# Generator blocks moved into the step, other first steps, and biases added tile by tile

## The reference

```
scale = cond @ norm_w.T + 1.0
h = x * (scale[:, None, :] * rsqrt(mean(x * x, -1) + 1e-6))
val, gate = split(h @ up_w.T, 2)                      # 2 x 1024 columns
h = val * gelu(gate)
y = act_quant(h) @ weight_quant(down_w).T + x         # rows to 8 bits, weights to -1, 0, 1

dWd = ((cond @ Wdd.T + bdd) * 0.1).reshape(B, 128, 256)
dWu = ((cond @ Wdu.T + bdu) * 0.1).reshape(B, 256, 128)
down = relu(y @ (Wd + dWd).T + bd)                    # weights of its own for each sequence
out = y + down @ (Wu + dWu).T + bu
```

## Time and profile before

| | us |
|---|---|
| median of three runs | 473.36 |
| the profiled execution, whole | 473.57 |
| its span, first to last instruction | 471.8 |
| PE busy in the span | 464.3 (98%) |
| VectorE busy | 386.4 (82%) |
| ScalarE busy | 364.3 (77%) |
| GpSimd busy | 269.1 (57%) |

### The profile page before, as it was taken

One profiled execution on the slowest core, in us unless ns is written; L12 is line 12 of the kernel. 1 busy time (PEld: TensorE's weight loads), 2 busy tenths in 40 slices (PEclk: granted clock), 3 DMA queues, 4 the chain that ended last, 5 costly groups with the idle time before them and its releaser, 6 DMA issues.

```text
span 471.8 us, 10035 instructions
## 1 busy us (share of the span) xinstructions
PE 464.3 (98%) x3276; PEld 269.3 (57%) x3276; DVE 386.4 (82%) x787; ACT 364.3 (77%) x636; POOL 269.1 (57%) x681
## 2 busy tenths in 40 slices
PE   8999999999999999999999999999999999999996
PEld 7445565665656555555555555555555555655564
DVE  3887798888989898788888887878888888777886
ACT  3788999999999967776777777686686787677664
POOL 1653558565675645465656546656555656544663
PEclk9999999999999999999999999999999999999999
DMA  7925588967778455535545445645535455444343
GB/s 259 392 80 111 135 206 200 260 182 217 182 236 243 104 103 120 106 100 162 130 133 157 91 124 136 166 122 136 137 84 162 124 145 147 113 105 119 101 81 110
DMA packets 118003, 70.99 MB, mean 150 GB/s; under 512 B 102016, under 2 KB 102976, under 8 KB 115904
## 3 DMA queue, kind: packets, MB, share of 16 engines
q1 hardware_dynamic: 117360, 69.63, 56.4%
q10 hardware_dynamic: 592, 0.73, 0.5%
HBM read 37.44 MB, written 8.39 MB: 97 GB/s over the span
## 4 chain that ended last, share of the span: by engine, by line
PE 91%; DVE 3%; DMA 1%; issue 1%; ACT 1%; POOL 1%; ACTq 0%; DVEq 0%; POOLq 0%
PE bank L1147 65%; PE bank L1161 11%; PE bank L1223 5%; PE bank L1255 4%; PE bank L1241 4%; DMA xT_s<-in_xT 1%; PE bank L1123 1%; PE bank L1129 1%; DVE up_lo L1020 0%; ACT gel L621 0%; DVE hid L857 0%; POOL nwt L463 0%; PE bank L1173 0%; DVE amax L865 0%; POOL rms L470 0%
## 5 line engine op out<-in xcount | busy, mean ns | idle before, releaser
L621 ACT ACTIVATE gel<-bank,rms 128x512 f32<-128x512 f32 x125 | 85.5, 685 | 87.3 <-PE bank L1147 84.4
L1147 PE MATMUL bank<-up_hi,xs_hi 128*128 128x512 f16 x492 | 146.3, 379 | 0.3 <-DVE hid L857 0.3
L1147 PE MATMUL bank<-up_lo,xs_hi 128*128 128x512 f16 x492 | 146.3, 379 | 0.0
L1147 PE MATMUL bank<-up_hi,xs_lo 128*128 128x512 f16 x492 | 146.3, 379 | 0.0
L857 DVE SCALAR_TENSOR_TENSOR hid<-bank,rms,gel 128x512 f32<-128x512 f32 x121 | 90.6, 749 | 62.3 <-ACT gel L621 61.5
L1147 PEld LDWEIGHTS bank<-up_lo,xs_hi 128*128 128x128 f16 x492 | 48.1, 98 | 58.1
L1147 PEld LDWEIGHTS bank<-up_hi,xs_lo 128*128 128x128 f16 x492 | 48.1, 98 | 58.0
L448 POOL TENSOR_TENSOR wsplit<-stage,wsplit 128x288 f16<-128x288 f32 x64 | 53.1, 859 | 42.1 <-ACT wsplit L593 42.1
L865 DVE TENSOR_REDUCE amax<-hid 128x1 f32<-128x1024 f32 x61 | 74.4, 1220 | 2.1
L634 ACT ACTIVATE hid<-hid,amax 128x1024 f32<-128x1024 f32 (+1 forms) x62 | 70.0, 1130 | 0.4 <-DVE amax L909 0.4
L1161 PE MATMUL bank<-tern,qT 128*128 128x256 bf16 x504 | 65.3, 273 | 0.8 <-DVE x L969 0.7
(11 more groups left out here) (145 smaller groups left out, 662.7 us busy)
## 6 DMA issues: line engine op xcount, KB each, us to landing
xn_s<-in_xn SPq DMA_DIRECT2D x32, 256.0 KB, 3.4
stage<-in_WddT SPq DMA_DIRECT2D x8, 1024.0 KB, 6.1
stage<-in_WduT SPq DMA_DIRECT2D x8, 1024.0 KB, 5.4
xT_s<-in_xT SPq DMA_DIRECT2D x31, 256.0 KB, 3.1
out<-out_s SPq DMA_DIRECT2D x30, 256.0 KB, 2.3
adapt<-in_up_wT SPq DMA_DIRECT2D x4, 512.0 KB, 7.8
x<-in_down_wT SPq DMA_DIRECT2D x2, 512.0 KB, 9.1
qT<-qn SPq DMA_TRANSPOSE x63, 2.7
```

What stands on the lines that cost most here:

```text
L621: nc.scalar.activation(gel_of(t, c), u_banks(t, c)[1][:], ACT.Gelu, scale=rms[:, t // TPB % XN_SLOTS, t % TPB:t % TPB + 1]).then_inc(gelu_ ...
L1147: ins = nc.tensor.matmul(dst[:], a[:, t // TPB % 2, k, cols], w[:, c, k, v, :], start=(k == 0 and n == 0), stop=(k == KD - 1 and n == 2))
```

## The change

The step loop of PE issues `generate(q)` between `down` and `up(s, 1)`, and in step 7 + q rather than at the end of step 6 + q. In the first two steps, `up_first` is cut in two: the passes with the weights' low parts become `up_first_end` and come later. Eleven idle matmuls stand ahead of the first real one rather than eight. The sum of the absolute weights moves from step 3 to step 2, with ACT's `absolute_sum`, DVE's `ternary_first` and `ternary_second` earlier; `squares(2)`, `squares(3)` and `rsqrt_guess(2)` are earlier as well. `base_sum` on POOL moves from the start to step 5. The first load of `xT` goes from ACT's queue to SP's, behind the first piece of the up weights. At the end, `output(B - 3)` on PE moves ahead of three transposes, `total(B - 3)` on DVE with it, and POOL adds the bias of sequence B - 2 one tile at a time, the first of them earlier.

```diff
@@ -69,7 +69,7 @@
 N_NEWTON = 11
 
 
-IDLE_FIRST = 8
+IDLE_FIRST = 11
 IDLE_SECOND = 7
 
 
@@ -395,6 +395,8 @@
             sp.dma_start(cond2[0:C, :], condT).then_inc(ld_cond, 16)
             for n in range(NC * KD):
                 sp.dma_start(raw_up[:, n // KD, n % KD], up_wT[:, n // KD, n % KD]).then_inc(ld_up[n], 16)
+                if n == 0:
+                    sp.dma_start(xT_s[:, 0], xT[0]).then_inc(ld_xT[0], 16)
             sp.dma_start(xn_s[:, 0], xn[0]).then_inc(ld_xn[0], 16)
             load_x(1)
             for i in range(2):
@@ -511,6 +513,12 @@
                     nc.gpsimd.tensor_tensor(out_s[:, b % OUT_SLOTS, i], x1[:, (b * TPB + i) % X1_SLOTS], bu_row[:], ALU.add
                                             ).then_inc(outb_done, 1)
 
+            def output_bias_tile(b, i):
+                pool.wait_ge(x1_done, b * TPB + i + 1)
+                pool.wait_ge(stored[b % OUT_SLOTS], 16 * (b // OUT_SLOTS))
+                nc.gpsimd.tensor_tensor(out_s[:, b % OUT_SLOTS, i], x1[:, (b * TPB + i) % X1_SLOTS], bu_row[:], ALU.add
+                                        ).then_inc(outb_done, 1)
+
             def base_sum():
                 pool.wait_ge(ld_base, 16 * N_BASE)
                 nc.gpsimd.tensor_scalar(bias_raw, bias_raw, DELTA_SCALE, None, ALU.mult).then_inc(base_ready, 1)
@@ -545,7 +553,6 @@
 
             split_cond()
             rsqrt(1)
-            base_sum()
             rsqrt(2)
             for t in range(FIRST - 2):
                 dequantization(t)
@@ -559,6 +566,8 @@
                     low_part(q)
                 for b in scales(s):
                     rsqrt(b)
+                if s == FIRST + 1:
+                    base_sum()
                 if s == LAST_T - 1:
                     residual_low(LAST_T - 4)
                 for b in adapter_splits(s):
@@ -567,11 +576,12 @@
                     identity()
             output_bias(B - 3)
             dequantization(LAST_T - 1)
+            output_bias_tile(B - 2, 0)
             residual_low(LAST_T - 3)
             middle_low(B - 4)
             dequantization(LAST_T)
             residual_low(LAST_T - 2)
-            output_bias(B - 2)
+            output_bias_tile(B - 2, 1)
             middle_low(B - 3)
 
             pool.wait_ge(x1_lo_done, LAST_T - 2)
@@ -697,7 +707,6 @@
                                          scale=1.0 / A_SCALE).then_inc(relu_done, 1)
 
             act.dma_start(normw, norm_wT).then_inc(ld_cond, 16)
-            act.dma_start(xT_s[:, 0], xT[0]).then_inc(ld_xT[0], 16)
             act.dma_start(cond2[C:2 * C, :], condT).then_inc(ld_cond_again, 16)
             act.wait_ge(const_ready, 2)
             nc.scalar.activation(warm[:], zero[:], ACT.Gelu)
@@ -715,18 +724,18 @@
             squares(0)
             scaled_high(1)
             squares(1)
+            absolute_sum(0)
             gelu(0, 0)
             gelu(0, 1)
             gelu(1, 0)
+            absolute_sum(1)
             gelu(1, 1)
-            absolute_sum(0)
-            absolute_sum(1)
+            squares(2)
             gelu(2, 0)
             quantize(0)
             quantized(0)
             gelu(2, 1)
             scaled_high(2)
-            squares(2)
             gelu(3, 0)
             quantize(1)
             quantized(1)
@@ -738,8 +747,8 @@
                     relu(b)
                 gelu(s, 0)
                 if s == FIRST:
+                    squares(3)
                     gelu(s, 1)
-                    squares(3)
                 quantize(s - 1)
                 if s < LAST_T:
                     for t in split_tiles(s):
@@ -1029,16 +1038,16 @@
             quant_scale(0)
             gate(1, 0)
             gate(1, 1)
+            ternary_first()
             gate(2, 0)
+            rsqrt_guess(2)
             quant_scale(1)
             gate(2, 1)
-            ternary_first()
+            ternary_second()
             gate(3, 0)
-            rsqrt_guess(2)
             scaled_low(2)
             quant_scale(2)
             gate(3, 1)
-            ternary_second()
             ternary_third()
             for s in range(FIRST, NT):
                 if s == LAST_T:
@@ -1083,9 +1092,9 @@
             residual_high_last()
             residual_low(LAST_T)
             residual_low(LAST_T - 1)
+            total(B - 3)
             x63_lo_evacuate()
             x62_evacuate()
-            total(B - 3)
             split_last()
             total(B - 2)
             total_last()
@@ -1122,6 +1131,10 @@
                         for v, dst in enumerate(u_banks(t, c)):
                             nc.tensor.matmul(dst[:], a[:, 0, k, cols], up_hi[:, c, k, v, :],
                                              start=(k == 0 and n == 0), stop=False)
+
+            def up_first_end(t, c):
+
+                cols = slice(t * P, (t + 1) * P)
                 for k in range(KD):
                     if t == 0:
                         pe.wait_ge(up_ready, c * KD + k + 1)
@@ -1288,17 +1301,24 @@
                 if s < TPB:
 
                     up_first(0, s)
+                    if s == 1:
+                        up_first_end(0, s)
                     up_first(1, s)
+                    if s == 0:
+                        up_first_end(0, s)
+                    up_first_end(1, s)
                     continue
-                if s == 3:
+                up(s, 0)
+                if s == 2:
 
                     pe.wait_ge(hid_done, NC + 1)
                     pe.wait_ge(absum_ready, 2)
                     nc.tensor.matmul(sum_ps, ones[:], wsum[:, 0:1], start=True, stop=False)
                     nc.tensor.matmul(sum_ps, ones[:], wsum[:, 3:4], start=False, stop=True).then_inc(absum_full, 1)
-                up(s, 0)
                 for t in downs(s, 0):
                     down(t)
+                for q in chunk(s, 2):
+                    generate(q)
                 if s < LAST_T:
                     up(s, 1)
                 else:
@@ -1306,8 +1326,6 @@
                     up_last(1)
                 for t in downs(s, 1):
                     down(t)
-                for q in chunk(s, 1):
-                    generate(q)
                 for b in outputs(s):
                     output(b)
                 for b in sequences(s, 0):
@@ -1320,6 +1338,7 @@
             down_last()
             pe.wait_ge(late_lo_done, 3)
             x_transpose(LAST_T - 2, x61_ps, (0, 1))
+            output(B - 3)
 
             pe.wait_ge(last_x1_hi_done, 1)
             x_transpose(LAST_T, x63_hi_ps, (0,))
@@ -1328,7 +1347,6 @@
             x_transpose(LAST_T, x63_lo_ps, (1,))
             pe.wait_ge(x1_lo_done, LAST_T - 2)
             x_transpose(LAST_T - 1, x62_ps, (0, 1))
-            output(B - 3)
             middle_last(1)
             middle_last(0)
             output(B - 2)
```

## The result

The changed kernel takes 481.11 us (median of four runs, 480.92 to 482.01), the kernel before, beside it, 473.41. The ratio is 1.0166, with a 95% interval of 1.0149 to 1.0184: slower by 7.7 us, where +4.5 was forecast and the range ended at 479.4. The profiled execution of the changed kernel took 480.92 us with a span of 479.2; before, 473.57 and 471.8.

A forecast was written before the change was run, and what follows sets the result against it. PE, busy for 98% of the span, was taken as the bound. The terms 6.7 - 0.8 - 1.15 - 0.3 = +4.5 us took the profiled 473.57 to 478.1, so 477.9 us was predicted, range 476.2 to 479.4.

The forecast's parts named there:

- The chain behind the third pass: PE waits for `xs_lo` in tiles 8 to 22, T ending the previous even step's second half: eight times, 6.7 us.
- The 0.84: PE's forecast wait for `xs_lo` at each third pass, in us, from T + 8.31 to T + 9.15.
- the 0.13: Forecast delay in us from the end of `xs_lo` until PE goes on.
- Blocks: Generator blocks on PE no longer wait for POOL's low part: -0.8 us, bounds -0.8 and 0.
- Steps 2 to 6: PE's early stalls shrink through earlier roots, squares and ACT work: -1.15 us, bounds -1.7 and 0.
- The first steps and the idle matmuls: Start of PE: -0.3 us for the wait for `up_lo`, 0 for the three more idle matmuls.
- the same bytes stood in both queues before, so I take 0: Load of `xT` on SP's queue: second piece of weights 0 to 0.6 us later, taken as 0.
- The idle term: Three more idle matmuls before PE's first real one: taken as 0, bounds 0 and +0.65 us.
- The 0.3 for the low pass of the first steps: PE's wait for `up_lo` goes, with tile 1's eight matmuls ahead: -0.3 us, bounds -0.3 and 0.
- The end: `output(B - 3)` moves into a gap of PE: taken as 0, bounds -0.65 and +0.2 us.
- The first rival: The `xs_lo` chain at the third pass stays hidden and the change wins: 471.1 us, chance 0.07.
- The second rival: Clock stays low through the idle loops (+0.65), early stalls only change place (+1.15): 479.7 us, chance 0.13.

The follow-up runs named there:

- the version without waits: The changed kernel with sequence 27's store ahead of tile 62's transpose on SP and `scaled_low` ahead of the evacuations on DVE: 470.11 us, ratio 0.9930.

## Why the prediction was wrong, step by step

The direction was right and so was the main mechanism; the time lies 1.7 us above the range because of a wait at the end that I did not look for.

- *The chain behind the third pass*, right: `xs_lo` at T + 9.02 was forecast and T + 9.00 measured, PE's arrival T + 8.31 and T + 8.32, eight times. The 0.84 was mis-sized: PE goes on 0.05 us behind `xs_lo`; the 0.13 was read at the start, and doesn't hold in the steps. 8 x 0.73 = 5.8, inside the bounds of 5.7 to 7.8.
- *Blocks*, right: -0.8 forecast; 0.71 in the change's trace (5.8 - 5.09), 0.80 in the version without waits. The prediction's words count one block too many: in the trace before, the first block is late by 0.2, three by 0.17 and one by half of that, and this gives the 0.8.
- *Steps 2 to 6*, right: -1.15 forecast, -1.15 in the trace, and 1.14 again when the orders are put back.
- *The first steps and the idle matmuls*, too small a gain: -0.3 forecast, -1.15 in the trace. One step that failed is "the same bytes stood in both queues before, so I take 0", with bounds of 0 to 0.6 on the other side. I looked at the second piece of weights, which did not come later: it landed at 8.40 to 9.33 us in the traces with the load on SP's queue, at 9.46 and 9.40 in the two without. What PE waits for first is `xs_lo`, made from `xT`, and `xT` landed at 7.19 to 8.12 us in the former and at 8.22 and 8.44 in the latter. The idle term, bounded by 0 below, was a gain in this execution: the matmuls came at the full rate by the second loop, though the runs leave open whether three idles more did that. In the late starts it was a loss inside its bound: `up(2, 0)` 0.46 later than before. The 0.3 for the low pass of the first steps is not shown by any run.
- *The end. "I take 0 (bounds -0.65 and +0.2)"* is the step that failed, and it alone put the time outside the range. I followed `output(B - 3)` and left out the other edit at the end, the two calls of `output_bias_tile`. They move a wait for `stored` ahead of `residual_low` and `middle_low` on POOL, and asking what is queued behind them there would have found it. Price against before: 3.66 us of wait and 0.87 in the tail, where some 1.6 of lower clock are in part paid back. The two runs that took the wait away, on POOL or on SP, won 4.2 and 4.9 us and took 476.9 and 476.2 us. That this lies in the range, at its lower edge, is partly luck: the start gained 0.85 more than forecast and the eight waits cost 0.9 less.
- The first rival (chain hidden, 471.1) did not happen, but a hidden chain is what the version with `scaled_low` first has: 470.11. The second rival's time, 479.7, is the nearest, but for other reasons: neither of its two losses occurred in the traced execution, and the first of them shows only in the late starts.

## What to carry to other kernels

When an instruction is moved forward on an engine's queue, its waits are moved forward with it, for all that stands behind. Follow every one of them to its producer's queue as well: here a store with its data ready stood behind a transpose that was not. Work taken out from behind a producer and put ahead of it shortens the time that hid that producer's chain, so work out which wait ends last at the new place; reordering the producer's own queue (`xs_lo` ahead of the evacuations on DVE) may cost nothing. And a stall of PE of some microseconds costs more than itself when the clock falls behind it.

## What the runs showed of the hardware

- The clock's fall after an idle PE varies: behind the same 3.7 us stall PE ran at full rate until about 466.5 in the change's trace, and was already at 0.50 when it went on with the blocks put back. With idle matmuls in the gap it stayed at 1.00.
- At the start the moment of the rise differs from one execution to the next: PE's first real matmul stood between 7.98 and 10.41 us in kernels with the same 11 idles. There only the distance of the matmuls tells it; the granted clock of the window from 5 to 8 us is given as 1.00 in both cases. By the Trainium skill, page "TensorE: Matmul & The Clock Gate", section "What's actually happening", that moment varies from run to run; the traces agree.
- DVE instructions with two inputs in SBUF have two durations: `xs_lo` takes 0.48 us alone and 0.95 beside POOL's large tensor instructions, with a few between (0.54 to 0.91). Moving it up to where POOL makes a chunk's low part lengthened it from 0.86 to between 1.45 and 1.78 us a pair, and it still came 0.18 to 0.51 us before PE. The first such pair, tile 8's:

```profile
56.51 1.60 DVE L849 SCALAR_TENSOR_TENSOR xs_lo<-xT_s,scaleT,xs_hi 128x256 f16<-128x256 f32 x2
...
L849 DVE SCALAR_TENSOR_TENSOR xs_lo<-xT_s,scaleT,xs_hi x64: 468/576/977, 8.3 to 440.9; 128x256 f16<-128x256 f32 x64
```

The second line is that operation's own view: least, median and longest ns of its 64 instructions. By the Trainium skill, page "SBUF — State Buffer", section "Who interferes with whom", a VectorE instruction with two inputs in SBUF contends with a GpSimd instruction that reads SBUF; the two durations agree with it, and no run here separates it from other causes.
